# Layer 0 of a two-layer transformer block: the q and k projection in tiles of seven 18-column groups

## The reference

```
ada = silu(c) @ W_ada + b_ada            # shift, scale, gate, twice
h = layernorm(x) * (1 + scale) + shift
q, k, v = split(h @ W_qkv + b_qkv)       # 16 heads of 18 columns each
x = x + gate * (softmax(q * 18**-0.5 @ k.T) @ v @ W_proj + b_proj)
x = x + gate2 * (gelu(modulate(layernorm(x)) @ W_fc1 + b_fc1) @ W_fc2 + b_fc2)
```

## Time and profile before

| | us |
|---|---|
| median of 3 runs | 995.5 (993.51 to 996.24) |
| the profiled execution | 996.99 |
| its span, first to last instruction | 995.2 |
| TensorE busy | 857.5 (86%) |
| VectorE busy | 659.8 (66%) |
| ScalarE busy | 540.9 (54%) |
| GpSimd busy | 285.5 (29%) |

### The profile page before, as it was taken

How to read it: one execution, slowest core, us unless ns; L and a number is a source line. 1 busy time by engine, 2 the same in 40 slices (tenths; PEclk the granted TensorE clock), 3 DMA queues, 4 the chain that set the end, 5 groups by cost and what they waited for, 6 DMA issues and landing times. The chain is left out here.

```text
span 995.2 us, 16869 instructions
## 1 busy us (share of the span) xinstructions
PE 857.5 (86%) x6204; PEld 387.7 (39%) x6204; DVE 659.8 (66%) x1278; ACT 540.9 (54%) x763; POOL 285.5 (29%) x339
## 2 busy tenths in 40 slices
PE   3798999999999999998887999995778874699996
PEld 1361122222222222222154646653445553455564
DVE  1868888888888888888068554553279768655521
ACT  1471577777777777777956324441456623355530
POOL 1512112223454421110045315223023446321222
PEclk9897799999999999999989999997899987799998
DMA  8000010111102100000500100001564540100000
GB/s 266 9 16 21 19 25 25 25 43 42 43 20 64 27 19 19 19 19 1 135 0 1 37 24 2 0 1 41 135 135 122 132 109 5 31 1 25 24 24 25
DMA packets 49615, 43.11 MB, mean 43 GB/s; under 512 B 23394, under 2 KB 40068, under 8 KB 49543
## 3 DMA queue, kind: packets, MB, share of 16 engines
q1 hardware_dynamic: 49543, 42.15, 16.2%
HBM read 25.45 MB, written 9.44 MB: 35 GB/s over the span
## 5 line engine op out<-in xcount | busy, mean ns | idle before, releaser
L816 DVE TENSOR_REDUCE row_max<-ps 128x1 f32<-128x512 f32 x512 | 324.5, 685 | 68.3 <-PE ps L1491 67.1
L1273 ACT ACTIVATE probs<-ps 128x1024 f32<-128x1024 f32 x256 | 248.5, 1017 | 45.2 <-PE ps L1518 44.9
L1491 PE MATMUL ps<-stack_area 54*128 54x512 f16 x512 | 161.3, 394 | 26.6 <-DVE row_max L816 21.2
L1530 PE MATMUL ps<-probs,mlp_area 128*32 128x512 f32 x1024 | 136.5, 605 | 0.5 <-ACT probs L1273 0.5
L1491 PEld LDWEIGHTS ps<-stack_area 54*128 54x128 f16 x512 | 40.4, 93 | 192.9 <-DVE row_max L816 172.1
L1518 PE MATMUL ps<-stack_area 56*128 56x512 f16 x512 | 110.2, 384 | 5.4 <-ACT probs L1273 5.1
L1616 PE MATMUL ps<-w_fc,mlp_area 128*128 128x288 f16 x864 | 108.9, 289 | 5.9 <-DVE mlp_area L939 5.9
L1603 PE MATMUL ps<-mlp_area,w_fc 128*128 128x512 f16 x504 | 110.4, 379 | 3.6 <-DVE v_sb L793 1.7
L1312 ACT ACTIVATE mlp_area<-ps 128x512 f32<-128x512 f32 x72 | 43.0, 597 | 116.3 <-PE ps L1603 115.3
L1616 PEld LDWEIGHTS ps<-w_fc,mlp_area 128*128 128x128 f16 x864 | 84.7, 99 | 29.4 <-DVE mlp_area L939 5.8
L625 POOL TENSOR_SCALAR neg_scaled<-neg_max 128x16 f32<-128x16 f32 x16 | 4.1, 254 | 277.5 <-DVE neg_max L823 277.5
(11 more groups left out here) (165 smaller groups left out, 1177.8 us busy)
## 6 DMA issues: line engine op xcount, KB each, us to landing
qkv_rows<-part_area SPq DMA_DIRECT2D x24, 252.0 KB
stack_area<-tokens SPq DMA_DIRECT2D x128, 36.0 KB
x_sb<-in_x SPq DMA_DIRECT2D x4, 576.0 KB, 14.1
stack_area<-part_area SPq DMA_DIRECT2D x64, 36.0 KB
w_raw<-in_L_cond_W_fc SPq DMA_DIRECT2D x4, 576.0 KB
w_raw<-in_L_cond_fc_w SPq DMA_DIRECT2D x4, 576.0 KB
tokens<-qkv_rows SPq DMA_DIRECT2D x64, 36.0 KB
v_sb<-qkv_rows SPq DMA_DIRECT2D x16, 144.0 KB
```

What stands on the lines that cost most here:

```text
L816: nc.vector.reduce_max(row_max[:, p % 2, t, j, half:half + 1], bank(bk), AX.X).then_inc(max_done, 1)
L1273: nc.scalar.activation(probs[:, n % 2, 2 * c:2 * c + 2, :].rearrange("p h n -> p (h n)"), ps[:, 2 + 2 * c:4 + 2 * c, :].rearrange("p b n - ...
L1491: nc.tensor.matmul(bank(bk), stacks[rows, p % RING, 0, t * P:(t + 1) * P], stacks[rows, p % RING, 1, half * 512:(half + 1) * 512], start=T ...
L1530: mm = nc.tensor.matmul(bank(6)[at:at + VW, :], v_pad[:, TB * (p // BPAIR) + n, 2 * (p % BPAIR) + j, :], probs[:, n % 2, 2 * c + j, :], st ...
```

## The change

The q and k weights of layer 0 lie densely, 576 columns of interleaved 18-column groups (q of head 0, k of head 0, q of head 1, ...). A projection tile takes seven groups, 126 columns, and the last one of a batch four groups, 72 columns. A batch has five tiles in place of eight, both batches ten in place of 16, each again in two halves of seven matmuls. A pair's four groups lie in one tile or in two. Tile n is projected in the slots of the first pair that needs it; those first pairs are 0, 1, 3, 5, 7 and 8, 9, 11, 13, 15. So pairs 2, 4, 6, 10, 12 and 14 have no P step, no ScalarE copies and no GpSimd split of their own. The 12 DMAs a pair stay; they read from the group's own rows. Since q and k rows now mix, the scale 18**-0.5 moves from the copy into the exponential. The memset of the zero fields is gone, and the buffers behind `w_qk` move forward.

```diff
+PG = P // D
+PROWS = PG * D
+BPARTS = -(-2 * H // PG)
+NPART = 2 * BPARTS
-PART_SCALE = (QS * UN * D ** -0.5, QS * UN)
-        w_qk = tokens16[:, 5 * B * L:5 * B * L + 5 * BPAIR * P].rearrange("p (k a n) -> p k a n", k=5, a=BPAIR)
+        w_qk = tokens16[:, 5 * B * L:5 * B * L + 5 * 2 * C].rearrange("p (k n) -> p k n", k=5)
...
+        def part_rows(n):
+            return min(PROWS, 2 * C - PROWS * (n % BPARTS))
+        def part_place(p, x, j):
+            u, g = divmod(2 * (2 * (p % BPAIR) + j) + x, PG)
+            return BPARTS * (p // BPAIR) + u, D * g
+        def parts_used(p):
+            return sorted({part_place(p, x, j)[0] for x in range(2) for j in range(2)})
+        FIRST_PAIR = [min(p for p in range(NPAIR) if n in parts_used(p)) for n in range(NPART)]
+        PAIRS_OF = [[p for p in range(NPAIR) if n in parts_used(p)] for n in range(NPART)]
...
-                if rest == 0 and 0 < p < NPAIR:
-                    return [("P", p, c)]
+                if rest == 0 and p > 0 and p in FIRST_PAIR:
+                    return [("P", FIRST_PAIR.index(p), c)]
...
-                sp.wait_ge(part_done, p + 1)
+                sp.wait_ge(part_done, parts_used(p)[-1] + 1)
...
-                        if p + 2 < NPAIR:
-                            split_part(p + 2)
+                        if p + 2 in FIRST_PAIR:
+                            split_part(FIRST_PAIR.index(p + 2))
...
-                nc.scalar.activation(part_f[:, 512 * c:512 * (c + 1)], bank(bk), ACT.Copy, scale=part_scale[:, 0:1]
+                nc.scalar.activation(part_f[rows, 512 * c:512 * (c + 1)], bank(bk)[rows], ACT.Copy, scale=QS * UN
...
-                        ACT.Exp, scale=1.0 / (QS * QS)).then_inc(probs_ready, 1)
+                        ACT.Exp, scale=D ** -0.5 / (QS * QS)).then_inc(probs_ready, 1)
...
-                    mm = nc.tensor.matmul(bank(bk), w_qk[:, w, p % BPAIR, :], hT_all[:, a, t0:t0 + 512],
+                    mm = nc.tensor.matmul(bank(bk)[0:rows], w_qk[:, w, row:row + rows], hT_all[:, a, t0:t0 + 512],
```

More of the change, by code:

```diff
@@ L28 @@
 HROWS = 64
-SW = 32
+PG = P // D
+PROWS = PG * D
+BPARTS = -(-2 * H // PG)
+NPART = 2 * BPARTS
 KR = 3 * D
@@ L91, in hidden_blocks_kernel @@
         silu_t = sb("silu_t", [96, 3 * B])
-        part_scale = sb("part_scale", [P, 1])
         tokens16 = tokens[:].bitcast(F16)
         hT_all = tokens16[:, 0:5 * B * L].rearrange("p (k n) -> p k n", k=5)
-        w_qk = tokens16[:, 5 * B * L:5 * B * L + 5 * BPAIR * P].rearrange("p (k a n) -> p k a n", k=5, a=BPAIR)
-        tail = tokens[:, (5 * B * L + 5 * BPAIR * P) // 2:]
+        w_qk = tokens16[:, 5 * B * L:5 * B * L + 5 * 2 * C].rearrange("p (k n) -> p k n", k=5)
+        tail = tokens[:, (5 * B * L + 5 * 2 * C) // 2:]
         part_f = tail[:, 0:L]
@@ L207, in hidden_blocks_kernel @@
         stack_in = [sem(f"stack_in{i}") for i in range(RING)]
-        part_cols = sem("part_cols")
         ones_set, row_in = sem("ones_set"), sem("row_in")
@@ L398, in heads_of @@
         def heads_of(dst, x):
-            return dst.rearrange("p a (x j s) -> p a x j s", x=2, j=2)[:, :, x, :, 0:D]
+            return dst.rearrange("p (h x d) -> p x h d", x=2, d=D)[:, x]
         def columns_of(src, x):
-            return src[:, C * x:C * (x + 1)].rearrange("p (a j d) -> p a j d", j=2, d=D)
+            return src[:, C * x:C * (x + 1)].rearrange("p (h d) -> p h d", d=D)
         block = ctx.enter_context(nc.Block())
@@ L411, in load_ada @@
                 if l:
-                    sp.wait_ge(part_mm, QC * NPAIR)
+                    sp.wait_ge(part_mm, QC * NPART)
                 sp.dma_start(ada_w_sb[l], ada_w[l].rearrange("(k p) n -> p k n", p=96)).then_inc(ada_in, 16)
@@ L444, in store_stacks @@
             def store_stacks(p):
-                sp.wait_ge(part_done, p + 1)
+                sp.wait_ge(part_done, parts_used(p)[-1] + 1)
                 if p >= RING:
                     sp.wait_ge(scores_ready, QC * SLOTS * (p - RING + 1))
-                hi, lo = part_hi[p % 2], part_lo[p % 2]
-                for x, copies in enumerate(((hi, lo, hi), (hi, hi, lo))):
+                for x in range(2):
                     for j in range(2):
-                        first = HROWS * x + SW * j
-                        for i, src in enumerate(copies):
+                        n, first = part_place(p, x, j)
+                        hi, lo = part_hi[n % 2], part_lo[n % 2]
+                        for i, src in enumerate((hi, hi, lo) if x else (hi, lo, hi)):
                             to = HROWS * j + D * i
@@ L608, in invert, with split_part @@
                                         power[:], ALU.pow).then_inc(rstd_ready, 1)
[L610 to L617, removed]
+            def split_part(n):
+                rows = slice(0, part_rows(n))
+                pool.wait_ge(part_taken, QC * (n + 1))
+                if n > 1:
+                    for p in PAIRS_OF[n - 2]:
+                        pool.wait_ge(*stacked(p))
+                nc.gpsimd.tensor_copy(part_hi[n % 2][rows], part_f[rows]).then_inc(part_high, 1)
+                pool.wait_ge(part_high, n + 1)
+                nc.gpsimd.tensor_tensor(part_lo[n % 2][rows], part_f[rows], part_hi[n % 2][rows], ALU.subtract
+                                        ).then_inc(part_done, 1)
             def split_maxima(p):
@@ L662, in _ @@
             chain(nc.gpsimd.memset(power[:], -0.5))
-            pads = w_qk.rearrange("p k a (x s) -> p (k a x) s", s=SW)
-            nc.gpsimd.memset(pads[:, :, D:SW], 0.0)
             nc.gpsimd.memset(max_rows_sb[0:MR, :], ONE_ROW).then_inc(ones_set, 1)
@@ L752, in _ @@
             nc.vector.memset(eps_pair[:, 1:2], EPS).then_inc(const_ready, 1)
-            for x in range(2):
-                nc.vector.memset(part_scale[HROWS * x:HROWS * (x + 1), :], PART_SCALE[x]).then_inc(part_cols, 1)
             dve.wait_ge(const_ready, 1)
@@ L1065, in _ @@
                     attention()
-                    dve.wait_ge(part_mm, QC * NPAIR)
+                    dve.wait_ge(part_mm, QC * NPART)
                     spread_cond(1)
@@ L1244, in take_hT, with take_part @@
                                      ACT.Copy).then_inc(hT_ready[ph], 1)
[L1246 to L1252, removed]
-                nc.scalar.activation(part_f[:, 512 * c:512 * (c + 1)], bank(bk), ACT.Copy, scale=part_scale[:, 0:1]
+            def take_part(n, c, bk):
+                rows = slice(0, part_rows(n))
+                if n:
+                    act.wait_ge(part_done, n)
+                act.wait_ge(part_mm, QC * n + c + 1)
+                nc.scalar.activation(part_f[rows, 512 * c:512 * (c + 1)], bank(bk)[rows], ACT.Copy, scale=QS * UN
                                      ).then_inc(part_taken, 1)
@@ L1476, in value_mms, with part_mms @@
                 mm.then_inc(v_mm, 1)
-            def part_mms(p, c, bk, first, end):
-                t0 = L * (p // BPAIR) + 512 * c
+            def part_mms(n, c, bk, first, end):
+                t0 = L * (n // BPARTS) + 512 * c
+                row, rows = PROWS * (n % BPARTS), part_rows(n)
                 for i in range(first, end):
                     a, w = PRODUCTS[i]
-                    mm = nc.tensor.matmul(bank(bk), w_qk[:, w, p % BPAIR, :], hT_all[:, a, t0:t0 + 512],
+                    mm = nc.tensor.matmul(bank(bk)[0:rows], w_qk[:, w, row:row + rows], hT_all[:, a, t0:t0 + 512],
                                           start=(i == 0), stop=(i == len(PRODUCTS) - 1))
```

## The result

| | before | after |
|---|---|---|
| median (runs) | 995.84 (4) | 986.77 (4, 985.32 to 989.04) |
| ratio, 95% interval | | 0.9916 (0.9887 to 0.9944) |
| profiled execution | 996.99 | 985.32 |
| its span | 995.2 | 983.4 |

The change takes 9.1 us off the median (by the interval 5.6 to 11.3) and 11.7 off the profiled execution. 11.5 off and 984.0 were forecast. The median 986.8 lies inside the forecast's range of 980.5 to 989.0, 2.8 above its value. First come the page's groups of the kernel after (busy us and mean ns, idle before and its releaser), then weight loads by shape between 112 and 470 us.

The account below looks back on a forecast made before the run. It took TensorE to bound the P slots, with VectorE nearly the bound in cycles without P. Its terms, -13.6 + 0 + 1.4 + 0.7 = -11.5 us, took the median of 995.5 to 984.0, range 980.5 to 989.0.

Parts of the forecast that it names:

- Ten chunks, -13.6: Slots 8 to 93: removing five chunks of each half, at 1.10 and 1.62 us, saves 13.6 us.
- half 1 alone: Attention loop: an eight-slot cycle keeping only its half-1 chunk takes 24.40 us, against 25.50 with both.
- half 0 alone: Attention loop: an eight-slot cycle keeping only its half-0 chunk takes about 23.9 us, against 25.50 with both.
- rival A: Attention loop: P was hidden by VectorE, so nothing comes back and the time stays 995.5; chance 6%.
- in a P slot TensorE is the bound: Attention loop's P slots: TensorE has no gap, while VectorE waits 1.32 us for S matmuls behind the P matmuls.
- Loads, +1.4: Remaining chunks from slot 0 on: 126-column weight loads, 12 chunks with three open loads of 0.039 us more, cost 1.4 us.
- 72 columns load as fast as 128: Tiles 4 and 9: their 72-column weights load in 78 ns by proportion, no more than now.
- Pair 9's stack, +0.7: Pair 9's first S: the faster loop makes it wait for its stack DMA, +0.7 us, from 0 to 1.6.
- Rival B: Attention loop: stack supply becomes the bound, DMAs or splits 2 to 3 us later, time 990.1; chance 10%.
- Slots before the first exponential, 0: Slots -8 and -4: pair 2's removed matmuls were hidden by VectorE, so 0 us, bounded by -2 and +3.
- Rival C: Loop's P slots: lighter TensorE lets the granted clock fall, 2.6 us more per such slot, time 1004.8; chance 5%.
- Behind the loop, 0: From 500 us on: everything only starts earlier by the same amount, so 0 us of its own.

Follow-up runs that it names:

- cols128: Changed kernel with weight loads of 128 columns in place of 126, tiles starting at the same columns; median 982.1 us.
- p_back5: Changed kernel with the projection matmuls of pairs 4, 6, 10, 12 and 14 back on TensorE alone, no copies or splits; median 999.7 us.
- p_one: Changed kernel with only one of the seven products in every chunk of tiles 1 to 9, q and k wrong; median 971.1 us.
- p_behind: Changed kernel with the P slot reordered: weigh, both first S, then all seven projection matmuls in one row; median 990.9 us.
- job_later: Changed kernel with each weight job of layer 0 loaded and split one pair later (FIRST_JOB = 2); median 986.0 us.
- three: Changed kernel with 128-column weight loads, weight jobs one pair later, and pair 2's projection matmuls back on TensorE alone; median 983.0 us.
- p_back2: Changed kernel with pair 2's 14 projection matmuls back in slots -8 and -4 on TensorE alone; median 984.5 us.
- spread: Changed kernel with three of each chunk's seven matmuls, and ScalarE's copy, one slot later; median 997.5 us.
- three_spread: Changed kernel with 128-column weight loads, weight jobs one pair later, and chunks cut over two slots, without pair 2's matmuls; median 995.6 us.

## Why the prediction was right

*Ten chunks, -13.6.* Right, and for the reason given: half 1 alone was forecast at 24.40 and half 0 alone at 23.88, and without the slower loads they are 24.40 and 23.89 (cols128). p_back5 shows that copies and splits have no part in it, and the cycles contradict rival A. What I had not seen is what p_one shows: the price of a chunk is not in proportion to its matmuls; the first of the seven alone costs 0.84 us in half 1. And "in a P slot TensorE is the bound" was too simple: p_behind shortened TensorE's slot by 0.60 us and the cycle grew. The forecast held because whole chunks were removed, and the trace of before had priced whole chunks.

*Loads, +1.4.* Right in size: cycles 1 to 13 carry 1.4 us, and cols128 took 1.2 of it back (in cycle 8 the wait for the stack hid some 0.1). The chunk in cycle 0, which the term had counted in, adds 0.22 at the lower clock, so the term comes to 1.6. The forecast that 72 columns load as fast as 128 was off (111 ns and not 78), which changes 4 of 16 chunks by 0.04 us.

The Trainium skill ("TensorE: Matmul & The Clock Gate", weight-path perf modes) ties the fast load to exactly 128 weights. cols128 bears it out: 97 ns with 128 columns, 134 with 126, in the same place of the same loop. The formula of its section "LDWEIGHTS (loading the stationary operand)", P/1.2 ns for P columns, halved for the fast load, would have had 105 and 53 ns, both well under the measured ones.

*Pair 9's stack, +0.7.* Right: 0.7 in cycle 8, gone in job_later. Rival B is the same mechanism a few us further on; in p_one it takes 2.1 us.

*Slots before the first exponential, 0.* The term that was off, though inside its bounds: +0.67. VectorE did hide the removed matmuls: the second scores start at 104.17, 104.16 before. Then TensorE's clock rose later, which is 0.41 of the 0.67; 0.22 is the loads at the lower clock. From 76.9 to 96.9 us, where the earlier trace rows has a clock of 0.77, the kernel after has 0.63 (from 84 to 97 alone 0.50, 0.64 before), and it was still at 0.50 after 111.3. The prediction had bounded this term because a lighter TensorE might shift the rise; that it did is not shown (p_back5 and three against p_back2). Rival C, a clock that falls in the loop, did not happen: from 120 to 460 us it stayed at 1.00.

*Behind the loop, 0.* The profiled execution gained 1.0 us there, by no step of mine. From the last maxima to the end of the span the kernels' profiled executions take 518.4 us (cols128) to 525.7 (p_behind), 521.4 before and 520.4 after, with the same program there. So differences of 1 to 2 us in the totals, such as the 9.1 us between the medians against 11.7 between the profiled executions, or cols128's 4.7, are not to be read as the change's. That the 11.7 lies so close to the forecast 11.5 is in part luck: the ledger of the loop gives 10.8, and the 1.0 behind it was not forecast.

## What to carry to other kernels

When a loop runs out of one kind of work before it ends, its last cycles price that work; this trace had the answer to 0.02 us a cycle before anything was changed. Where the matmuls stand in the slot counts as well as how many there are: from cycle 1 on, four, two S, three takes 4.05 us less than two, S, two, S, three, and two S, seven takes 3.7 more (medians 979.1, 986.8 and 990.9). And a stretch that differs from kernel to kernel with the same program, like cycle 0 here, needs more than one trace before its change is given a cause. Last, check which supply chain is next: the margin of 0.7 us at pair 9 was readable beforehand and became a wait as soon as the loop was faster.

## What the runs showed that I had not expected

- Cutting a chunk over two slots made it dearer, by 0.74 us (24.50 to 25.24) and 0.89 (24.00 to 24.89). More room for VectorE in the P slot is no gain where the next slot has none.
- The moment at which the granted clock leaves 0.50 in the first slots lies between about 108 and 113 us, and cycle 0 is 22.19 to 24.79 us over these kernels. It differs between kernels with the same order of matmuls there (spread 24.03, three_spread 22.53; after 24.27, p_back5 23.70), so what sets it stays open.
- 72 weight columns load in 111 ns, more than 128 columns with 97.
